# VectorE's work beside the expert loop in smaller pieces: norm in 14 slots instead of 7, routing in 30 instead of 20

## The chip, the cores and the metric

One core of one Trainium2 chip runs the whole program in one launch. The metric is the device time of one execution in microseconds (us); given are the median and the extremes of several runs. The engines are PE (TensorE, matmuls), DVE (VectorE), ACT (ScalarE), POOL (GpSimd) and SP (SyncE, which only issues transfers). Each works through its own list of instructions in order; semaphores alone tie the lists together.

## The reference

The input is x of 2 x 1024 tokens of 128 features. Four layers follow one another, and each adds to x:

```
x += attention_a(layernorm(x))   # full, 16 heads of 8, 1024 keys
x += experts(layernorm(x))
x += attention_b(layernorm(x))   # banded, 32 keys back
x += experts(layernorm(x))       # same weights

experts(x): shared = silu(x sg^T) * (x su^T) sd^T
  scores  = sigmoid(x gate^T) + gate_bias            # 64 experts, 8 groups of 8
  mask    = the 4 groups with the largest maximum
  comb    = the 6 largest masked scores, divided by their sum, 0 elsewhere
  routed  = sum over experts e of comb[e] * (silu(x eg[e]^T) * (x eu[e]^T)) ed[e]
```

Every token goes through every expert; `comb` is the weight, mostly zero. So what is called routing here is the making of the weights `comb` for 1024 tokens: norm, logits, two rounds of "keep the largest k, ties by position", and a normalisation.

## The kernel before, in words

The tokens are two batches of 1024 (8 tiles of 128 tokens, `TB = 8`). The 64 experts and 2 shared ones stand in 33 pairs (`PAIRS`). `experts` runs once per expert layer (names M1ex and M2ex) and is one loop over 132 steps q: step q works on pair q // 2 and on half a batch (512 tokens, c = q % 2); the first 66 steps (`HB`) are batch 0, the rest batch 1. In one step

- PE does `gate_up(q)`, 6 matmuls of 512 columns into two banks of a ring of three, and `down(q - 3)`, 3 more. `gate_up(q)` waits for `hid_ready` of step q - 2, since it writes the bank that DVE then has read;
- ACT does `silu(q)` and a cast to 16 bits (`high_part(q - 1)`);
- DVE does `times_up(q)` and `times_weight(q)` (the rows `ring` and `hid`), the second one with the weights of the pair (`cb`), which SP fetches per pair from the DRAM array `comb`;
- POOL makes the low half, `low`, from `hid` and `high`.

Beside the first 66 steps the same engines prepare batch 1: the attention's output projection, norm and routing. This work is written as generators, and each engine's loop calls `next(beside)` once per step, on DVE behind `times_weight(q)`. What a generator does between two `yield`s is called a **slot** or a **piece** here. The slots tie the engines together only by count: 13 slots for the projection (steps 0 to 12), then `NORM_SLOTS` and `ROUTE_SLOTS`. PE's transposes of the normed tiles are in the last two slots of the norm, POOL's reciprocal root in the slot in which DVE asks for it, PE's transposes of `comb` in the last two slots of the routing, DVE's last routing piece one slot ahead of them. In M1ex a second norm, of batch 0 for the next attention, is called from step 74 on (`AFTER`). Batch 1's weights are written to DRAM by `store_weights` on SP, inside SP's loop over pairs p, and pair 33 is the first that reads them. The same generators run without a loop, one piece straight after another, at the end of the first attention (on DVE) and in `first_batch` of the second expert layer.

Of the kernel before, what the change touches and what calls it, by code (L numbers as in the profile page):

```python
# [83 lines left out]
def attend_full(nc, env, tag):  # L84
# [10 lines left out]
    with ExitStack() as ctx:  # L95
# [566 lines left out]
def start(nc, env, d):  # L662
# [4 lines left out]
    with ExitStack() as ctx:  # L667
# [78 lines left out]
        def _(dve):  # L746
# [9 lines left out]
            for _ in range(3):  # L756
                next(norm)
# [312 lines left out]
def norm_of_batch_vector(dve, env, n, b, bank=None):  # L1070

    x = lambda t: env.x[:, TB * b + t, :]
    for t in range(TB):
        dve.bn_stats(n.stats[:, t, :], x(t)).then_inc(n.step, 1)
        if t == TB // 2 - 1:
            yield
    yield
# [4 lines left out]
    dve.tensor_scalar(n.ve[:, :], n.mv[:, :, 1], EPS, None, ALU.add).then_inc(n.var_ready, 1)
    yield
# [20 lines left out]
def norm_of_batch_gpsimd(pool, env, n):  # L1104


    for _ in range(3):
        yield
# [3 lines left out]
    for _ in range(4):  # L1112
# [101 lines left out]
def route_gpsimd(pool, env, n, q, b):  # L1214
# [18 lines left out]
def route_vector(dve, env, q):  # L1233
# [637 lines left out]
```

## Time and profile before

| | |
|---|---|
| median of 3 runs | 1254.93 us (1249.84 to 1260.67) |
| profiled execution, its own time | 1258.97 us |
| its span, first to last instruction | 1257.1 us |
| busy: PE, DVE, ACT, POOL | 1082.9, 960.0, 686.8, 423.0 us |
| mean granted clock of PE | 0.897 of full speed |
| M1ex loop | 453 to 752 us |
| M2ex loop | 966 to 1254 us |
| transfer of one pair's weights, issue to landing (median) | 4.0 us |

The profile lists what each engine did and when; a "granted clock" of 1.00 is 2.4 GHz, 0.50 is 1.2 GHz. Busy time is an average over stages with different limits: what the change is worth must be read inside the two expert loops. In a timeline row a bracket such as [0.36 <-ACT M1ex_sil L1648] says how long the engine had been idle before the instruction, and which instruction it had waited for.

### The profile page before, as it was taken

To read this page: it belongs to the slowest core of one execution; us is meant where nothing else is said; L and a number is where in the kernel's file an instruction comes from. 1 tells how busy PE (TensorE), PEld (TensorE's weight loads), DVE (VectorE), ACT (ScalarE), POOL (GpSimd) and SP (SyncE) were. 2 spreads that over 40 slices of the span, in tenths; PEclk is the share of its full clock that TensorE was granted. 3 is DMA by queue.
4 is the path that set the end of the run, shared out by engine and by line. 5 is a ranking of instruction groups with operands and counts; after the bars stand their busy time and mean duration, and the time that the engine had idled before them with its cause. 6 is when DMAs were issued, how large, how long until landed. Compare 5 with 4: busy or idle time off the path is not lost. (4 is left out here: it accounts for less than half of the span.)

```text
span 1257.1 us, 18664 instructions
## 1 busy us (share of the span) xinstructions
PE 1082.9 (86%) x6278; PEld 435.3 (35%) x6278; DVE 960.0 (76%) x2188; ACT 686.8 (55%) x1047; POOL 423.0 (34%) x352
## 2 busy tenths in 40 slices
PE   6586999999999988989989993688854988999998
PEld 4111222222222334434444441233342543444443
DVE  8599999999998567787767765777335768777775
ACT  2103787778777854656655651345512555666665
POOL 3004055322000124555545550000001555555654
PEclk8555999999999989999999996689755999999999
DMA  8220022202200144557747833121012646667662
GB/s 316 53 50 26 20 53 73 73 21 52 50 1 7 34 124 130 156 144 193 184 116 200 210 78 100 47 59 54 3 38 65 166 120 157 186 189 197 187 188 64
DMA packets 72903, 131.62 MB, mean 105 GB/s; under 512 B 13400, under 2 KB 48344, under 8 KB 72808
## 3 DMA queue, kind: packets, MB, share of 16 engines
q1 hardware_dynamic: 70320, 122.50, 36.6%
q10 hardware_dynamic: 2488, 7.93, 1.8%
q8 instruction: 50, 0.82, 0.3%
q14 instruction: 45, 0.37, 0.1%
HBM read 115.08 MB, written 14.91 MB: 103 GB/s over the span
## 5 line engine op out<-in xcount | busy, mean ns | idle before, releaser
L374 DVE TENSOR_REDUCE Aatt_mx<-Aatt_sc 128x1 f32<-128x512 f32 x512 | 317.7, 684 | 25.7 <-PE Aatt_sc L222 25.2
L325 ACT ACTIVATE Aatt_prob<-Aatt_st 128x1024 f32<-128x1024 f32 x256 | 247.7, 1022 | 77.4 <-PE Aatt_st L231 76.7
L222 PE MATMUL Aatt_sc<-ks,qs 48*128 48x512 bf16 x512 | 171.8, 430 | 42.8 <-DVE Aatt_mx L374 20.5
L1755 POOL TENSOR_TENSOR M1ex_low<-M1ex_hid,M1ex_high 128x512 f16<-128x512 f32 x132 | 153.6, 1164 | 149.8 <-ACT M1ex_high L1654 72.3
L1755 POOL TENSOR_TENSOR M2ex_low<-M2ex_hid,M2ex_high 128x512 f16<-128x512 f32 x132 | 153.6, 1164 | 136.5 <-PE M2ex_acc L1610 81.9
L1648 ACT ACTIVATE M2ex_sil<-M2ex_ring,unscale 128x512 f32<-128x512 f32 x132 | 90.7, 687 | 96.9 <-PE M2ex_ring L1593 96.8
L1648 ACT ACTIVATE M1ex_sil<-M1ex_ring,unscale 128x512 f32<-128x512 f32 x132 | 90.7, 687 | 95.7 <-PE M1ex_ring L1593 95.4
L242 PE MATMUL Aatt_pv<-Aatt_prob,vg 128*32 128x512 f32 x1024 | 141.0, 623 | 0.6 <-ACT Aatt_prob L325 0.6
L1692 DVE SCALAR_TENSOR_TENSOR M2ex_ring<-M2ex_ring,unscale,M2ex_sil 128x512 f32<-128x512 f32 x132 | 100.1, 758 | 48.8 <-ACT M2ex_sil L1648 44.6
L1692 DVE SCALAR_TENSOR_TENSOR M1ex_ring<-M1ex_ring,unscale,M1ex_sil 128x512 f32<-128x512 f32 x132 | 100.0, 757 | 48.5 <-ACT M1ex_sil L1648 44.0
L222 PEld LDWEIGHTS Aatt_sc<-ks,qs 48*128 48x128 bf16 x512 | 37.4, 95 | 240.0 <-DVE Aatt_mx L374 217.7
L231 PE MATMUL Aatt_st<-qs,ks 51*128 51x512 bf16 x512 | 106.7, 393 | 3.6 <-ACT Aatt_prob L325 2.6
L1702 DVE TENSOR_TENSOR M2ex_hid<-M2ex_ring,M2ex_cb 128x512 f32<-128x512 f32 x132 | 91.3, 692 | 15.5
L1702 DVE TENSOR_TENSOR M1ex_hid<-M1ex_ring,M1ex_cb 128x512 f32<-128x512 f32 x132 | 91.3, 692 | 15.5
L625 DVE CUSTOM_DVE_ANT_0 Batt_sc<-Batt_sc,mask 128x160 f32<-128x160 f32 (+1 forms) x256 | 74.3, 353 | 36.7 <-PE Batt_sc L515 36.7
L1654 ACT CAST M1ex_high<-M1ex_hid 128x512 f16<-128x512 f32 x132 | 80.5, 610 | 25.3 <-DVE M1ex_hid L1702 23.2
L1654 ACT CAST M2ex_high<-M2ex_hid 128x512 f16<-128x512 f32 x132 | 80.4, 609 | 18.4 <-DVE M2ex_hid L1702 17.0
L602 ACT ACTIVATE Batt_prob<-Batt_st 128x320 f32<-128x320 f32 x128 | 49.0, 435 | 55.9 <-PE Batt_st L566 55.9
L190 POOL COPY vg<-vn 128x256 f32<-128x256 f32 x8 | 3.2, 398 | 186.5 <-PE Aatt_pv L242 181.3
L1591 PE MATMUL M1ex_ring<-M_xh,M_wt 128*128 128x512 f16 x132 | 51.1, 387 | 10.5 <-DVE M1ex_hid L1702 5.5
L1591 PE MATMUL M2ex_ring<-M_xh,M_wt 128*128 128x512 f16 x132 | 50.7, 384 | 8.5 <-DVE M2ex_hid L1702 5.0
L515 PE MATMUL Batt_sc<-ks,qs 48*128 48x160 bf16 (+1 forms) x256 | 34.3, 267 | 22.7 <-DVE Batt_m L625 14.7
(423 smaller groups left out, 1863.4 us busy)
## 6 DMA issues: line engine op xcount, KB each, us to landing
M1ex_cb<-comb SPq DMA_DIRECT2D x130, 256.0 KB, 4.0
M2ex_cb<-comb SPq DMA_DIRECT2D x130, 256.0 KB, 3.9
M_wt<-wsplit SPq DMA_DIRECT2D x132, 192.0 KB, 3.9
wsplit<-split_cut SPq DMA_DIRECT2D x9, 704.0 KB, 4.5
qs<-stack SPq DMA_DIRECT2D x32, 96.0 KB
ks<-stack SPq DMA_DIRECT2D x30, 96.0 KB
split_raw<-in_wg_dram ACTq DMA_DIRECT2D x3, 704.0 KB, 7.0
split_raw<-in_wu_dram ACTq DMA_DIRECT2D x3, 704.0 KB, 13.3
```

The costliest lines, as they stand in the source:

```text
L222: pe.matmul(sc_bank(k, i)[:, :], qs[k][rows, jp, qt * P:(qt + 1) * P], ks[k][rows, jp, h * CH:(h + 1) * CH], start=True, stop=True).then_i ...
L231: mm = pe.matmul(st[jp][:, half, :], ks[k][rows, jp, kc * P:(kc + 1) * P], qs[k][rows, jp, qh * CH:(qh + 1) * CH], start=True, stop=True)
L242: mm = pe.matmul(pv[32 * j:32 * j + 32, :], vg[k][:, kc, j, :], prob[(2 * s + j % PAIR) % 4][:, j // PAIR, :], start=kc == 0, stop=kc == T ...
L325: act.activation(prob[e % 4][:, :, :].rearrange("p a c -> p (a c)"), st[pr][:, :, :].rearrange("p a c -> p (a c)"), ACT.Exp, scale=SCALE). ...
L374: dve.tensor_reduce(mx[k][:, m, part // 2:part // 2 + 1], sc_bank(k, i)[:, :], AX.X, ALU.max).then_inc(red_done, 1)
L625: ins = dve.tensor_tensor_reduce(scores, scores, mask_q[:, first:BAND], -1.0, -BARRED, ALU.add, ALU.min, accum_out=m1[k][:, j, qt:qt + 1])
L1591: pe.matmul(gate(q)[:, :], wt[k][:, 0, :], env.xh[:, cs], start=True, stop=False)
L1648: act.activation(sil[q % 2][:, :], gate(q)[:, :], ACT.Silu, scale=env.unscale[:, 0:1]).then_inc(sil_ready, 1)
L1654: act.copy(high[q % 3][:, :], hid[q % 3][:, :]).then_inc(high_ready, 1)
L1692: dve.scalar_tensor_tensor(up(q)[:, :], up(q)[:, :], env.unscale[:, 1:2], sil[q % 2][:, :], ALU.mult, ALU.mult).then_inc(up_ready, 1)
L1702: dve.tensor_tensor(hid[q % 3][:, :], up(q)[:, :], cb[k][:, c * CH:(c + 1) * CH], ALU.mult).then_inc(hid_ready, 1)
L1755: pool.tensor_tensor(low[q % 3][:, :], hid[q % 3][:, :], high[q % 3][:, :], ALU.subtract).then_inc(low_ready, 1)
```

## The change

DVE's pieces of norm and routing are cut smaller and stand in more slots; PE, ACT and POOL count to the new slots. POOL's root stays in slot 7, and DVE now takes it up one slot later, not in the same one. PE's transposes now stand two slots behind what they need, not one. The comparisons "greater", "equal" and the scan over experts are each split in two halves of 4 tiles. The end of the first attention keeps the old counts (7 and 20) on PE and ACT. On SP the store of batch 1's weights moves from pair 29 to just ahead of the fetch for pair 33. Core of the diff (calls that only pass the counts on are left out):

```diff
+OUT_SLOTS, NORM_SLOTS, ROUTE_SLOTS = 3 * ROUNDS_OUT + 1, 14, 30
+SHORT_NORM, SHORT_ROUTE = 7, 20
-OUT_SLOTS, NORM_SLOTS, ROUTE_SLOTS = 3 * ROUNDS_OUT + 1, 7, 20
@@ norm_of_batch_vector
         dve.bn_stats(n.stats[:, t, :], x(t)).then_inc(n.step, 1)
-        if t == TB // 2 - 1:
+        if t % 2:
             yield
-    yield
     dve.wait_ge(n.step, TB)
     for t in range(TB):
         dve.bn_aggr(n.mv[:, t, :], n.stats[:, t, :]).then_inc(n.step, 1)
+        if t == TB // 2 - 1:
+            yield
     dve.wait_ge(n.step, 2 * TB)
     dve.tensor_scalar(n.ve[:, :], n.mv[:, :, 1], EPS, None, ALU.add).then_inc(n.var_ready, 1)
     yield
+    yield
     dve.wait_ge(n.root_ready, 1)
...
     dve.wait_ge(n.step, 2 * TB + 3)
+    yield
     for t in range(TB):
...
-        if t in (1, 4):
+        if t % 2:
             yield
@@ norm_of_batch_gpsimd
-    for _ in range(3):
+    for _ in range(6):
         yield
     pool.wait_ge(n.var_ready, 1)
@@ route_gpsimd
-    for _ in range(ROUTE_SLOTS - 9):
+    for _ in range(16):
         yield
     pool.wait_ge(q.inv_ready, 1)
@@ route_vector: best() yields after 4 of its 8 dve.max; pick():
-        goes_on(dve.tensor_tensor(k.gt[:, :, :], values[:, :, :], wide(kth, n), ALU.is_gt))
-        yield
-        done(dve.tensor_tensor(k.eq[:, :, :], values[:, :, :], wide(kth, n), ALU.is_equal))
-        goes_on(dve.tensor_reduce(k.quota[:, :], k.above[:, :, 0:top], AX.X, ALU.add))
-        yield
-        done(dve.tensor_tensor_scan(flat(k.rank), flat(fresh), flat(k.eq), 0.0, ALU.mult, ALU.add))
+        for h in parts:
+            goes_on(dve.tensor_tensor(k.gt[:, h, :], values[:, h, :], wide(kth[:, h], n), ALU.is_gt))
+            yield
+        for h in parts:
+            goes_on(dve.tensor_tensor(k.eq[:, h, :], values[:, h, :], wide(kth[:, h], n), ALU.is_equal))
+            yield
+        dve.wait_ge(q.step, count[0])
+        done(dve.tensor_reduce(k.quota[:, :], k.above[:, :, 0:top], AX.X, ALU.add))
+        for h in parts:
+            goes_on(dve.tensor_tensor_scan(flat(k.rank[:, h, :]), flat(fresh[:, h, :]), flat(k.eq[:, h, :]), 0.0,
+                                           ALU.mult, ALU.add))
+            yield
         done(dve.tensor_scalar(k.quota[:, :], k.quota[:, :], -1.0, float(top), ALU.mult, ALU.add))
-        yield
         done(dve.tensor_tensor(k.keep[:, :, :], k.rank[:, :, :], wide(k.quota[:, :], n), ALU.is_le))
+        yield
         done(dve.tensor_tensor(k.keep[:, :, :], k.keep[:, :, :], k.eq[:, :, :], ALU.mult))
@@ experts, sync
                 sp.wait_ge(hid_ready, 2 * (p - CB_RING) + 2)
+                if p == PAIRS:
+                    store_weights(sp, env, q1, 1)
                 weights(p)
...
-                if p == PAIRS - 4:
-                    store_weights(sp, env, q1, 1)
```

DVE's list in M1ex, from the second group of `bn_stats` of the norm to the first normed tiles (`ring` and `hid` are the loop's own two operations, `r1`, `rstd` the steps behind POOL's root `r0`), before:

```order
L1074 BN_STATS M1exln_stats<-x_res 128x6 x4
L1692 SCALAR_TENSOR_TENSOR M1ex_ring1<-M1ex_ring1,unscale,M1ex_sil1 128x512
L1702 TENSOR_TENSOR M1ex_hid0<-M1ex_ring1,M1ex_cb2 128x512
L1080 BN_AGGR M1exln_mv<-M1exln_stats 128x2 x8
L1082 TENSOR_SCALAR M1exln_ve<-M1exln_mv 128x8
L1692 SCALAR_TENSOR_TENSOR M1ex_ring0<-M1ex_ring0,unscale,M1ex_sil0 128x512
L1702 TENSOR_TENSOR M1ex_hid1<-M1ex_ring0,M1ex_cb3 128x512
L1085 TENSOR_TENSOR M1exln_r1<-M1exln_r0 128x8
L1087 SCALAR_TENSOR_TENSOR M1exln_r1<-M1exln_r1,M1exln_ve 128x8
L1089 SCALAR_TENSOR_TENSOR M1exln_rstd<-M1exln_r1,M1exln_r0 128x8
L1092 TENSOR_SCALAR M1exln_xn<-x_res,M1exln_mv,M1exln_rstd 128x128 x2
```

and now, from the second half of the aggregation on:

```order
L1081 BN_AGGR M1exln_mv<-M1exln_stats 128x2 x4
L1085 TENSOR_SCALAR M1exln_ve<-M1exln_mv 128x8
L1703 SCALAR_TENSOR_TENSOR M1ex_ring0<-M1ex_ring0,unscale,M1ex_sil1 128x512
L1713 TENSOR_TENSOR M1ex_hid1<-M1ex_ring0,M1ex_cb4 128x512
L1703 SCALAR_TENSOR_TENSOR M1ex_ring2<-M1ex_ring2,unscale,M1ex_sil0 128x512
L1713 TENSOR_TENSOR M1ex_hid2<-M1ex_ring2,M1ex_cb0 128x512
L1089 TENSOR_TENSOR M1exln_r1<-M1exln_r0 128x8
L1091 SCALAR_TENSOR_TENSOR M1exln_r1<-M1exln_r1,M1exln_ve 128x8
L1093 SCALAR_TENSOR_TENSOR M1exln_rstd<-M1exln_r1,M1exln_r0 128x8
L1703 SCALAR_TENSOR_TENSOR M1ex_ring1<-M1ex_ring1,unscale,M1ex_sil1 128x512
L1713 TENSOR_TENSOR M1ex_hid0<-M1ex_ring1,M1ex_cb0 128x512
L1097 TENSOR_SCALAR M1exln_xn<-x_res,M1exln_mv,M1exln_rstd 128x128 x2
```

The root is asked for behind `ve`, and a whole step now stands between `ve` and `r1`; the normed tiles come in twos, a step later still.

DVE's list in M1ex round the scan (`rank`) over the experts, before:

```order
L1262 TENSOR_TENSOR M1exrt_experts_eq<-M1exrt_masked,M1exrt_experts_top8 128x512
L1263 TENSOR_REDUCE M1exrt_experts_quota<-M1exrt_experts_above 128x8
L1692 SCALAR_TENSOR_TENSOR M1ex_ring0<-M1ex_ring0,unscale,M1ex_sil0 128x512
L1702 TENSOR_TENSOR M1ex_hid1<-M1ex_ring0,M1ex_cb2 128x512
L1265 SCALAR_TENSOR_TENSOR M1exrt_experts_rank<-fresh,M1exrt_experts_eq 128x512
L1266 TENSOR_SCALAR M1exrt_experts_quota<-M1exrt_experts_quota 128x8
L1692 SCALAR_TENSOR_TENSOR M1ex_ring2<-M1ex_ring2,unscale,M1ex_sil1 128x512
L1702 TENSOR_TENSOR M1ex_hid2<-M1ex_ring2,M1ex_cb2 128x512
L1268 TENSOR_TENSOR M1exrt_experts_keep<-M1exrt_experts_rank,M1exrt_experts_quota 128x512
L1269 TENSOR_TENSOR M1exrt_experts_keep<-M1exrt_experts_keep,M1exrt_experts_eq 128x512
```

and now, from the first half of `eq` on:

```order
L1271 TENSOR_TENSOR M1exrt_experts_eq<-M1exrt_masked,M1exrt_experts_top8 128x256
L1703 SCALAR_TENSOR_TENSOR M1ex_ring2<-M1ex_ring2,unscale,M1ex_sil1 128x512
L1713 TENSOR_TENSOR M1ex_hid2<-M1ex_ring2,M1ex_cb3 128x512
L1271 TENSOR_TENSOR M1exrt_experts_eq<-M1exrt_masked,M1exrt_experts_top8 128x256
L1703 SCALAR_TENSOR_TENSOR M1ex_ring1<-M1ex_ring1,unscale,M1ex_sil0 128x512
L1713 TENSOR_TENSOR M1ex_hid0<-M1ex_ring1,M1ex_cb4 128x512
L1274 TENSOR_REDUCE M1exrt_experts_quota<-M1exrt_experts_above 128x8
L1276 SCALAR_TENSOR_TENSOR M1exrt_experts_rank<-fresh,M1exrt_experts_eq 128x256
L1703 SCALAR_TENSOR_TENSOR M1ex_ring0<-M1ex_ring0,unscale,M1ex_sil1 128x512
L1713 TENSOR_TENSOR M1ex_hid1<-M1ex_ring0,M1ex_cb4 128x512
L1276 SCALAR_TENSOR_TENSOR M1exrt_experts_rank<-fresh,M1exrt_experts_eq 128x256
L1703 SCALAR_TENSOR_TENSOR M1ex_ring2<-M1ex_ring2,unscale,M1ex_sil0 128x512
```

No piece now holds a whole scan, and `quota` (the small subtraction ahead of `keep`) has moved from the scan's piece to that of `keep`.

SP's list in M1ex round the store of batch 1's weights, before:

```order
L1548 DMA M1ex_cb<-comb 64x1024 [waits split_stored2]
L1548 DMA M1ex_cb<-comb 64x1024
L1426 DMA M_wt<-wsplit 128x768 [waits split_step]
L1210 DMA comb<-M1exrt_combT 66x512 [waits startqkv_v_done] x2
L1548 DMA M1ex_cb<-comb 64x1024 [waits split_stored2]
L1548 DMA M1ex_cb<-comb 64x1024
L1426 DMA M_wt<-wsplit 128x768 [waits split_step]
```

and now:

```order
L1559 DMA M1ex_cb<-comb 64x1024 [waits split_stored2]
L1559 DMA M1ex_cb<-comb 64x1024
L1437 DMA M_wt<-wsplit 128x768 [waits split_step]
L1212 DMA comb<-M1exrt_combT 66x512 [waits startqkv_v_done,split_stored2]
L1212 DMA comb<-M1exrt_combT 66x512 [waits startqkv_v_done]
L1559 DMA M1ex_cb<-comb 64x1024 [waits M1_comb_stored1]
L1559 DMA M1ex_cb<-comb 64x1024
L1437 DMA M_wt<-wsplit 128x768 [waits split_step]
L1559 DMA M1ex_cb<-comb 64x1024 [waits split_stored2]
```

The store stood several pairs ahead of the fetch that waits for it (`M1_comb_stored1`); now that fetch stands right behind it, with the weight matrices and all later pairs queued behind.

## Rows read from the trace of the kernel before

**Rows 1.** Busy time by stretch: us, PE, PEld, DVE, ACT, POOL, then clock, DMA.

```profile
487.07:557.51 70.44, 60.38 (x277) 27.21 (x276) 55.37 (x126) 38.09 (x62) 36.98 (x31) 0.95 0.51 140
502.20:505.90 3.70, 3.70 (x11) 1.43 (x11) 2.31 (x6) 1.35 (x4) 1.16 (x1) 0.50 0.67 194
582.77:606.08 23.31, 23.31 (x110) 10.55 (x109) 17.41 (x25) 14.31 (x25) 13.88 (x12) 1.00 0.73 187
624.43:645.75 21.32, 16.83 (x72) 7.55 (x71) 14.60 (x43) 9.88 (x17) 9.69 (x8) 0.92 0.49 131
999.51:1069.71 70.20, 60.02 (x277) 27.02 (x276) 55.34 (x126) 38.20 (x62) 36.97 (x31) 0.98 0.53 138
```

**Rows 2.** Timeline, DVE, undisturbed steps: start us, us, engine, line, operation.

```profile
581.72 0.69 DVE L1702 TENSOR_TENSOR M1ex_hid<-M1ex_ring,M1ex_cb 128x512 f32<-128x512 f32 x1
582.77 0.76 DVE L1692 SCALAR_TENSOR_TENSOR M1ex_ring<-M1ex_ring,unscale,M1ex_sil 128x512 f32<-128x512 f32 x1 [0.36 <-ACT M1ex_sil L1648]
```

**Rows 3.** Timeline, PE and POOL in the same step.

```profile
583.14 0.38 PE L1591 MATMUL M1ex_ring<-M_xh,M_wt 128*128 128x512 f16 x1
...
583.32 1.16 POOL L1755 TENSOR_TENSOR M1ex_low<-M1ex_hid,M1ex_high 128x512 f16<-128x512 f32 x1 [0.79 <-PE M1ex_acc L1610]
```

**Rows 4.** Chain of waits, second expert stage: start us, us, what.

```profile
1018.51 0.44 PE M2ex_side L1133 x4
...
1022.84 0.84 PE M2ex_side L1173 x8
```

**Rows 5.** Timeline, DVE, the norm of the first expert stage.

```profile
488.55 0.86 DVE L1074 BATCH_NORM_STATS2 M1exln_stats<-x_res 128x6 f32<-128x128 f32 x4
489.32 0.74 DVE L1692 SCALAR_TENSOR_TENSOR M1ex_ring<-M1ex_ring,unscale,M1ex_sil 128x512 f32<-128x512 f32 x1
...
498.94 0.17 DVE L1085 TENSOR_TENSOR M1exln_r<-M1exln_r 128x8 f32<-128x8 f32 x1 [3.57 <-POOL M1exln_r L1110]
...
499.55 0.60 DVE L1092 TENSOR_SCALAR M1exln_xn<-x_res,M1exln_mv,M1exln_rstd 128x128 f32<-128x128 f32 x2
```

**Rows 6.** Timeline, POOL and PE, in the same norm.

```profile
497.27 1.64 POOL L1110 TENSOR_TENSOR M1exln_r<-M1exln_ve,minus_half 128x8 f32<-128x8 f32 x1
...
499.95 0.73 PE L1133 MATMUL M1ex_side<-ident,M1exln_xn 128*128 128x128 f32 x2 [2.97 <-DVE M1exln_xn L1092]
```

**Rows 7.** Timeline, DVE and POOL round the experts' scan, first expert stage.

```profile
542.43 1.04 POOL L1225 TENSOR_TENSOR M1exrt_weighted<-M1exrt_masked,M1exrt_inv 128x512 f32<-128x512 f32 x1
...
542.78 1.78 DVE L1265 TENSOR_TENSOR_SCAN M1exrt_experts_rank<-fresh,M1exrt_experts_eq 128x512 bf16<-128x512 bf16 x1
...
543.70 1.80 POOL L1755 TENSOR_TENSOR M1ex_low<-M1ex_hid,M1ex_high 128x512 f16<-128x512 f32 x1 [0.22 <-POOL M1exrt_weighted L1225]
...
544.59 0.94 DVE L1266 TENSOR_SCALAR M1exrt_experts_quota<-M1exrt_experts_quota 128x8 f32<-128x8 f32 x1
```

**Rows 8.** By line, DVE: duration ns min/median/max, first and last start, shape.

```profile
L1265 DVE TENSOR_TENSOR_SCAN Aattrt_groups_rank<-fresh_g,Aattrt_groups_eq x1: 280/280/280, 436.7 to 436.7; 128x64 bf16<-128x64 bf16 x1
...
L1265 DVE TENSOR_TENSOR_SCAN Aattrt_experts_rank<-fresh,Aattrt_experts_eq x1: 1216/1216/1216, 443.3 to 443.3; 128x512 bf16<-128x512 bf16 x1
...
L1260 DVE TENSOR_TENSOR M1exrt_groups_gt<-M1exrt_gs,M1exrt_groups_top x1: 220/220/220, 523.1 to 523.1; 128x64 bf16<-128x64 f32 x1
...
L1260 DVE TENSOR_TENSOR M1exrt_experts_gt<-M1exrt_masked,M1exrt_experts_top x1: 685/685/685, 538.4 to 538.4; 128x512 bf16<-128x512 f32 x1
```

**Rows 9.** Timeline, DVE and PE, further pieces of the routing.

```profile
517.76 0.84 DVE L1278 SCALAR_TENSOR_TENSOR M1exrt_sc<-M1exrt_sc,gate_b 128x512 f32<-128x512 f32 x1
...
552.45 0.63 PE L1180 MATMUL M1ex_side<-ident,M1exrt_comb 128*66 128x128 f32 x4 [1.05 <-DVE M1exrt_comb L1303]
```

**Rows 10.** Timeline, SP: the weights' store and their reads.

```profile
448.78 0.90 SPq L1210 DMA_DIRECT2D comb<-split_raw  x2
...
453.08 1.15 SPq L1548 DMA_DIRECT2D M1ex_cb<-comb  x2
...
592.12 1.08 SPq L1548 DMA_DIRECT2D M1ex_cb<-comb  x2
```

More of the change, by code:

```diff
@@ L255, in first_batch @@
                 yield from out_tensor(pe, env, o, bank, 0)
-                yield from norm_of_batch_tensor(pe, env, n1, bank)
-                yield from route_tensor(pe, env, n1, q1, bank)
+                yield from norm_of_batch_tensor(pe, env, n1, bank, SHORT_NORM)
+                yield from route_tensor(pe, env, n1, q1, bank, SHORT_ROUTE)
             def second_batch():
@@ L334, in first_batch @@
             def first_batch():
-                for _ in range(OUT_SLOTS + NORM_SLOTS):
+                for _ in range(OUT_SLOTS + SHORT_NORM):
                     yield
-                yield from route_scalar(act, env, n1, q1, bank, 0, copies=False)
+                yield from route_scalar(act, env, n1, q1, bank, 0, copies=False, slots=SHORT_ROUTE)
             beside = first_batch()
@@ L1104, in norm_of_batch_gpsimd @@
 def norm_of_batch_gpsimd(pool, env, n):
-    for _ in range(3):
+    for _ in range(6):
         yield
@@ L1111, in norm_of_batch_gpsimd, with norm_of_batch_scalar @@
     pool.wait_ge(n.root_ready, 1)
-    for _ in range(4):
+    for _ in range(NORM_SLOTS - 6):
         yield
-def norm_of_batch_scalar(act, env, n, bank):
-    for _ in range(5):
+def norm_of_batch_scalar(act, env, n, bank, slots=NORM_SLOTS):
+    for _ in range(slots - 2):
         yield
@@ L1123, in norm_of_batch_scalar, with norm_of_batch_tensor @@
         yield
-def norm_of_batch_tensor(pe, env, n, bank):
-    for _ in range(5):
+def norm_of_batch_tensor(pe, env, n, bank, slots=NORM_SLOTS):
+    for _ in range(slots - 2):
         yield
@@ L1161, in route_buffers, with route_tensor @@
     return q
-OUT_SLOTS, NORM_SLOTS, ROUTE_SLOTS = 3 * ROUNDS_OUT + 1, 7, 20
-def route_tensor(pe, env, n, q, bank):
+def route_tensor(pe, env, n, q, bank, slots=ROUTE_SLOTS):
     for c in range(2):
@@ L1174, in route_tensor @@
         mm.then_inc(q.lg_done, 1)
-    for _ in range(ROUTE_SLOTS - 4):
+    for _ in range(slots - 4):
         yield
@@ L1182, in route_tensor, with route_scalar @@
         yield
-def route_scalar(act, env, n, q, bank, b, copies=True):
+def route_scalar(act, env, n, q, bank, b, copies=True, slots=ROUTE_SLOTS):
     for c in range(2):
@@ L1196, in route_scalar @@
                    scale=0.5).then_inc(q.sig_ready, 1)
-    for _ in range(ROUTE_SLOTS - 4):
+    for _ in range(slots - 4):
         yield
@@ L1228, in route_gpsimd @@
     pool.wait_ge(q.weighted_ready, 1)
-    for _ in range(7):
+    for _ in range(ROUTE_SLOTS - 18):
         yield
@@ L1290, in route_vector @@
     yield
-    best(of_experts, q.masked)
-    yield
+    yield from best(of_experts, q.masked)
     done(dve.tensor_reduce(q.total[:, :], of_experts.top8[:, :, 0:TOPK], AX.X, ALU.add))
@@ L1297, in route_vector @@
     yield
-    yield from pick(of_experts, q.masked, E, TOPK, env.fresh)
+    yield from pick(of_experts, q.masked, E, TOPK, env.fresh, HALVES)
     yield
@@ L1304, in route_vector @@
                       ALU.mult).then_inc(q.comb_ready, 1)
-    yield
-    yield
     yield
```

20 lines of the change are left out of this document (13 added, 7 removed).

## The prediction

> **What bounds the kernel now.** I read the busy times by stretch first. In an undisturbed part of an expert loop, 582.77 to 606.08 us, PE is busy for all 23.31 us at clock 1.00; these are 12 steps, so a step takes 1.94 us and PE sets it [rows 1]. Then the stretches that this change touches. Steps 13 to 39 of M1ex, norm and routing of batch 1, take 70.44 us, in M2ex 70.20 us; 27 steps at 1.94 are 52.4. PE has work of its own there that stays: two lots of four transposes of normed tiles at 0.44, two lots of logits at 0.84 [rows 4], and two lots of transposes of the weights, which I take at 0.44 too: 3.4 us. So **14.6 us in M1ex and 14.3 in M2ex are stalls**. Steps 74 to 80 of M1ex, the second norm, take 21.32 us [rows 1]; less 7 steps (13.6) and 0.9 for transposes, 6.8 are stalls. Together 35.7 us can be won, no more.
>
> Next, DVE's timeline, for what makes them. The step with four bn_stats (0.86) goes from 487.07 to 489.32, 2.25 us, and DVE doesn't idle behind it [rows 1, 5]. So DVE's own two operations with their gaps take 1.40, and **a piece of up to 0.54 us is free**; a longer one puts DVE behind by the rest. There is a reserve as well: hid ends at 582.41 (581.72 + 0.69), and PE, which waits for it, starts the bank's matmuls at 583.14 [rows 2, 3]. Allowing 0.05 for the semaphore, DVE may lag **0.68 us** before PE stands still, and it catches up 0.54 in each empty slot.
>
> The large stalls of before are then plain. In the norm DVE idles 3.57 us for POOL's root [rows 5]; PE stands 2.97 us before its transposes, behind the same root [rows 6], and is at clock 0.50 from 502.20 to 505.90, 3.70 us [rows 1]. In the routing the piece with the scan takes 1.78 + 0.94 [rows 7], and PE waits another 1.05 for the last piece [rows 9].
>
> **The change, norm.** Pairs of bn_stats (half of 0.86) and halves of the aggregation are under 0.54: free. The root: POOL starts it behind its low part of the same step. In an undisturbed step low ends at 583.32 + 1.16 = 584.48 [rows 3], 2.07 us behind the end of hid; the root takes 1.64 [rows 6], so it is there 3.71 behind that hid. Before, DVE came for it in the same step; now it comes a step, 1.94, later, and still idles 1.8. From r1 to the first normed tile it needs 0.61 (498.94 to 499.55 [rows 5]): a piece of 2.4, a lag of 1.87, a stall of 1.19 with the reserve gone. Four pieces of two normed tiles at 0.60 [rows 5] lag 0.06 each; the tail of POOL's low, 0.13 into each, may add as much, so 0.4. PE's transposes stand two slots behind their tiles: no wait there, and with PE idle for 1.2 instead of 3 us I expect no fall of the clock. Norm: **1.6 us left** of its stalls, three times.
>
> **The change, routing.** Half a comparison is estimated between 0.220 us at 64 elements and 0.685 at 512 [rows 8]: 0.42 at 256. Half a scan, between 0.280 and 1.216 [rows 8]: 0.68. Longest slots, as lag over 0.54 with 0.05 for a wait inside: the scores (0.84 [rows 9]) 0.36, group maxima 0.15 and masking 0.2 (as wide as the full comparison, 0.69), the four steps to the inverse 0.3, then free slots up to there and back to a lag of some 0.55. Now POOL forms the weighted scores, 1.04 us [rows 7], two steps behind the inverse, beside the first half of "equal". What that does rows 7 tell: weighted ends at 543.47, and the scan, started at 542.78, takes 1.78 instead of the 1.216 that it takes alone [rows 8], which is 0.56 more, as if it began at 543.34; POOL's low then takes 1.80 instead of 1.16; and quota, 0.94 for 8 elements, ends at 545.53, when low ends (545.50). They take turns, whole instructions at a time. So this slot is 1.0 longer than its 0.54: stall 0.9. The Trainium skill says the same in "SBUF — State Buffer", section "Who interferes with whom": VectorE and GpSimd share one pair of ports, and whoever issues first keeps it for the whole instruction. By that rule the sum holds as it stands; if they shared the bandwidth instead, that slot would cost about 0.1, and the result would be 1.6 us lower. Then, at full lag: maxima of the quota with half a scan (0.20 + 0.68) 0.35, second half 0.15, quota with keep (0.17 + 0.69) 0.45, the last piece 0.1. Routing: **1.9 left**, twice. The transposes of the weights, two slots behind, wait for nothing.
>
> **Sum.** First loop 14.6 − 1.6 − 1.9 = 11.1; second loop 14.3 − 3.5 = 10.8; second norm 6.8 − 1.6 = 5.2: 27.1 us. Against it: where DVE runs these steps alone, twice (end of the first attention, first_batch), three operations are now two each. Two halves of a comparison are 0.84 in duration against 0.685, of scans 1.36 against 1.216; most of the surplus overlaps, I take 0.3 us a pass, all on the path. The Trainium skill, "VectorE: DVE Perf Modes", section "The TRN2 errata", speaks against this change: each instruction pays a fixed latency, so tiles should be kept to 512 elements or more; with its formula, (N + 151) / 0.96 ns, an estimate for a half is 0.424 us. With that the three split pairs cost 0.47 a pass, and the result would be 0.3 us higher. At the start of the program DVE's order stays as it was. Net **−26.5 us**.
>
> The store on SP costs nothing in my sum. Its cover: the fetch for pair 33 is issued at 592.12 and its weights are used in step 66, 16.8 us later, of which the transfer takes 4.0. From store to the first read behind it took 4.3 us (448.78 to 453.08) [rows 10], so 8.5 are left, and the queue behind it (a matrix, then pair 34) is 5 pairs ahead.
>
> Against the profiled execution's own 1258.97 us the sum gives 1232.5. That execution is 4.0 above the median of the runs shown, 1254.93; so I forecast **1228.4 us**.
>
> **Rivals.**
> - *A (0.68), the forecast.* Own range 1223 to 1234, from what the residues could be: 7.0 of the 8.6 us left rest on the lag sums, and the three runs spread by 5 either way.
> - *B (0.12), the root stays dear.* If DVE lags when it asks, POOL lags with it, and the wait keeps more than 1.8 of its 3.57. For: POOL does low first, whatever the slot. Against: six pieces ahead of it are free. Price: up to 1.8 for each of three norms, 5.3, and if PE's stall then again lowers the clock, 1.85 each (3.70 us at half speed [rows 1]): 1234 to 1239.
> - *C (0.08), turns at the port everywhere.* DVE has some 14 pieces with two inputs per routing. If each met a POOL instruction as the scan did (0.6 to 0.8), 10 us per loop return: 1248. Against: in an undisturbed step low covers 583.32 to 584.48, and pieces stand mostly outside it. Meeting half of them gives 1238.
> - *D (0.08), nothing is left.* Pieces hide wholly, the root included: all 35.7 less 0.6: 1219.8. Against: the root's wait can't be shorter than low and root together.
> - *E (0.02), slower than before: the late store.* All of SP's list stands behind it. It decides from 12.8 us between store and first read; to return all 26.5 us it needs 13.3 more per loop, 26.1. At 30 it gives 1228.4 + 2 × 17.2 = 1262.8. Seen: 4.3.
> - *F (0.02), no effect.* If the slots of PE waited where DVE waits no more, 1250 to 1255. The list of DVE does change as the diff says, so this asks for a cause I don't see.
>
> **Numbers.** Less than 1% (12.5 us) can't be told from no change. Faster by more: A, B, D and over half of C, 0.93; within 1%: the rest of C, and F, 0.05; slower 0.02. The range for 8 in 10 takes A with its spread, B's lower half and D's edge: 1221 to 1238.
>
> **What would show it.** Right: steps 13 to 69 of each loop at 1.94 but for PE's own work; DVE's wait for the root at 1.8; clock 1.00 in the norm; no idle of PE before transposes of tiles or weights; the scan's halves near 0.68 and "quota" at 0.17; "equal", first half, near 1.4 for its turn behind weighted; cb of pair 33 landed before step 66. Wrong: a root wait near 3.5, a clock of 0.5 behind it, pieces lengthened beside low, or DVE idle for cb at step 66.

## The result, and the profile after

The changed kernel takes **1239.34 us** (median of 4 runs, 1234.83 to 1241.40) where the kernel before, run beside it, takes 1257.8: a ratio of 0.985, 95% interval 0.981 to 0.989. It is faster, as forecast, but by 18.5 us and not by 26.5, and the time lies 1.3 us above the range. The profiled execution took 1239.16 us with a span of 1237.3, 19.8 less than before.

First the stretches, by the windows view (columns as in [rows 1]). I cut each kernel at the first and the last of the 132 `ring` operations of an expert loop, since these are the loop's own clock. The kernel before, first loop, the stretch between the loops, second loop:

```profile
456.15:748.92 292.77, 277.35 (x1300) 130.61 (x1299) 223.40 (x396) 170.70 (x285) 157.74 (x135) 0.98 0.61 162
748.92:968.70 219.78, 143.94 (x1372) 67.71 (x1371) 122.35 (x680) 76.24 (x180) 12.55 (x15) 0.72 0.16 47
968.70:1247.35 278.65, 268.10 (x1268) 125.73 (x1267) 212.65 (x357) 164.15 (x275) 156.11 (x134) 0.99 0.63 167
```

and the changed kernel: the same three, then steps 13 to 26 (norm) and 27 to 56 (logits and routing) of M1ex, steps 74 to 87 (second norm), and the norm and the routing in M2ex:

```profile
455.68:734.96 279.28, 272.78 (x1300) 129.59 (x1299) 223.52 (x399) 170.74 (x285) 157.02 (x135) 0.99 0.67 170
734.96:957.83 222.87, 145.12 (x1373) 68.65 (x1372) 122.60 (x684) 76.22 (x180) 12.29 (x15) 0.71 0.16 46
957.83:1227.57 269.74, 266.19 (x1268) 125.23 (x1267) 212.26 (x361) 163.97 (x275) 155.45 (x134) 0.99 0.67 172
486.49:518.41 31.92, 29.93 (x136) 13.63 (x135) 25.59 (x56) 17.90 (x31) 17.78 (x15) 0.95 0.67 163
518.41:581.17 62.76, 61.87 (x296) 28.60 (x295) 53.90 (x107) 40.41 (x66) 38.16 (x33) 1.00 0.66 172
615.07:645.50 30.43, 28.32 (x135) 13.21 (x134) 25.49 (x57) 18.23 (x31) 17.80 (x15) 1.00 0.65 167
988.64:1020.55 31.91, 29.93 (x136) 13.62 (x135) 25.72 (x57) 17.90 (x31) 17.76 (x15) 0.95 0.61 161
1020.55:1082.95 62.40, 61.78 (x296) 28.61 (x295) 53.89 (x107) 40.39 (x66) 38.18 (x33) 1.00 0.67 173
```

The loops lost 13.5 and 8.9 us, **22.4 together, where 27.1 were forecast**; the stretch between them, where only the 0.3 us of one serial pass was charged, took 3.1 more. Inside the loops a step at PE's pace is 1.9425 us (23.31 us for 12 steps in [rows 1]). A norm has 14 steps and 0.88 us of PE's own work (its transposes), a routing 30 steps and 2.56 us (logits and transposes). With these taken off, the stalls that remain are: norms 31.92 − 27.2 − 0.88 = 3.84 in M1ex, 3.83 in M2ex, second norm 2.36; routing 62.76 − 58.3 − 2.56 = 1.9 and 1.6. So the routing is as forecast (3.5 for 3.8). **The norms keep 10.0 where 4.8 were forecast.**

Why, the timelines show. Changed kernel, DVE, the norm of M1ex at the root (answers to [rows 5]):

```profile
503.42 0.17 DVE L1089 TENSOR_TENSOR M1exln_r<-M1exln_r 128x8 f32<-128x8 f32 x1 [1.75 <-POOL M1exln_r L1115]
503.62 1.02 DVE L1091 SCALAR_TENSOR_TENSOR M1exln_r<-M1exln_r,M1exln_ve 128x8 f32<-128x8 f32 x1
504.68 0.17 DVE L1093 SCALAR_TENSOR_TENSOR M1exln_rstd<-M1exln_r 128x8 f32<-128x8 f32 x1
```

POOL, the same place (answers to [rows 6]):

```profile
501.75 1.64 POOL L1115 TENSOR_TENSOR M1exln_r<-M1exln_ve,minus_half 128x8 f32<-128x8 f32 x1
503.47 1.16 POOL L1766 TENSOR_TENSOR M1ex_low<-M1ex_hid,M1ex_high 128x512 f16<-128x512 f32 x1
```

The wait for the root is 1.75, as forecast (1.8; before 3.57). But the second small step behind it takes 1.02 us for 8 elements. In the same trace it takes 0.17 in the five norms outside the expert loops, where POOL has no `low` to start, and 1.02 in all three inside. It starts 0.15 behind POOL's `low` and ends (504.64) when `low` ends (504.63): POOL, freed of the root at the same moment as DVE, starts its late `low` at once, and the step waits for it to end. What PE makes of it:

```profile
504.13 0.38 PE L1621 MATMUL M1ex_acc<-M1ex_low,M_wt 128*128 128x512 f16 x1
506.50 0.39 PE L1602 MATMUL M1ex_ring<-M_xh,M_wt 128*128 128x512 f16 x1 [1.99 <-DVE M1ex_hid L1713]
...
507.19 0.63 PE L1607 MATMUL M1ex_ring<-M_xh,M_wt 128*128 128x512 f16 x1
...
509.75 0.63 PE L1602 MATMUL M1ex_ring<-M_xh,M_wt 128*128 128x512 f16 x1
...
510.57 0.38 PE L1604 MATMUL M1ex_ring<-M_xh,M_wt 128*128 128x512 f16 x1
```

PE stands 1.99 us, not 1.19, and then its matmuls take 0.63 instead of 0.38 from 507.19 to 510.17: the clock is at its lower level for some 3.4 us. In the second norm PE stood even longer, and the clock stayed at 1.00:

```profile
635.19 0.38 PE L1602 MATMUL M1ex_ring<-M_xh,M_wt 128*128 128x512 f16 x1 [2.10 <-DVE M1ex_hid L1713]
635.41 0.38 PE L1603 MATMUL M1ex_ring<-M_xl,M_wt 128*128 128x512 f16 x1
```

The routing, DVE at the experts' comparison and scan (answers to [rows 7, 8]):

```profile
559.30 0.48 DVE L1271 TENSOR_TENSOR M1exrt_experts_eq<-M1exrt_masked,M1exrt_experts_top 128x256 bf16<-128x256 f32 x1
...
561.17 1.04 DVE L1271 TENSOR_TENSOR M1exrt_experts_eq<-M1exrt_masked,M1exrt_experts_top 128x256 bf16<-128x256 f32 x1
...
563.85 0.69 DVE L1276 TENSOR_TENSOR_SCAN M1exrt_experts_rank<-fresh,M1exrt_experts_eq 128x256 bf16<-128x256 bf16 x1
...
567.98 0.16 DVE L1279 TENSOR_SCALAR M1exrt_experts_quota<-M1exrt_experts_quota 128x8 f32<-128x8 f32 x1
```

and POOL there:

```profile
559.46 1.23 POOL L1227 TENSOR_TENSOR M1exrt_weighted<-M1exrt_masked,M1exrt_inv 128x512 f32<-128x512 f32 x1
560.77 2.46 POOL L1766 TENSOR_TENSOR M1ex_low<-M1ex_hid,M1ex_high 128x512 f16<-128x512 f32 x2
```

The long turn came, but a step later than forecast and shorter: the first half of "equal" was already under way when `weighted` started, and it is the second half that waited, behind the `low` that `weighted` had delayed. That half takes 1.04, 0.5 over the free 0.54, where the prediction had near 1.4, 1.0 over it.

The store, SP's queue (answers to [rows 10]):

```profile
582.75 0.71 SPq L1212 DMA_DIRECT2D comb<-M1exrt_combT  x2
585.45 1.09 SPq L1559 DMA_DIRECT2D M1ex_cb<-comb  x2
...
587.21 1.08 SPq L1559 DMA_DIRECT2D M1ex_cb<-comb  x2
```

From the store to the first read behind it are 2.7 us; the fetch after it follows 1.76 us behind, so the queue catches up. DVE doesn't wait for the weights: its idle time before step 66 is 0.39 us, spent on ACT, and 0.36 to 0.39 before the steps beside it.

### The profile page after: what moved, and what is told of

The parts are those of the page before. It is cut to its first block and busy times, and to the rows that moved or that the text cites. A ratio compares the mean times of both kernels' runs of the same rounds, so it can differ in the third digit from the quotient of the medians.

```text
span 1237.3 us, 18676 instructions
## 1 busy us (share of the span) xinstructions
PE 1075.6 (87%) x6278; PEld 433.5 (35%) x6278; DVE 960.3 (78%) x2200; ACT 686.7 (56%) x1047; POOL 421.1 (34%) x352
## 5 line engine op out<-in xcount | busy, mean ns | idle before, releaser
L222 PE MATMUL Aatt_sc<-ks,qs 48*128 48x512 bf16 x512 | 171.4, 428 | 43.2 <-DVE Aatt_mx L374 19.8
L602 ACT ACTIVATE Batt_prob<-Batt_st 128x320 f32<-128x320 f32 x128 | 49.1, 436 | 57.8 <-PE Batt_st L566 57.8
L515 PE MATMUL Batt_sc<-ks,qs 48*128 48x160 bf16 (+1 forms) x256 | 34.5, 273 | 22.4 <-DVE Batt_m L625 14.1
```

The lines of the kernel that those rows point to most:

```text
L222: pe.matmul(sc_bank(k, i)[:, :], qs[k][rows, jp, qt * P:(qt + 1) * P], ks[k][rows, jp, h * CH:(h + 1) * CH], start=True, stop=True).then_i ...
```

## The experiments

Two theories of where the missing 5 us of the loops are. *R*: the price of the root is not only DVE's wait for it, but the turn that its followers lose to POOL's delayed `low`, and the fall of the clock that the longer stall brings at times; keep DVE away until root and `low` are through, and it is gone. *H*: the pieces themselves are too many or too long (halving, the collision in the routing). What a kernel's loops take is the sum of its two loop rows as above: before 571.4, changed 549.0.

**e1: the changed kernel again.**

> The changed kernel once more, on the same chip as the next three and in the same rounds. It separates what the change did inside the expert loops from what varies elsewhere: the stretch between the two expert loops (last ring row of M1ex to first ring row of M2ex), whose code the change hardly touches, was 219.8 us in the trace of before and 222.9 in the changed kernel's. If the 3.1 us are a variation of that stretch from execution to execution, its length differs again here and among the next three; if the change causes them (through the state in which the second attention starts), it stays near 222.9 here. The expert loops are expected within 0.5 us of the first trace (279.3 and 269.7 us from first to last ring row).

Measured: 1235.99 us, ratio 0.986 (0.982 to 0.990); loops 546.9. Norm of M1ex, and PE behind the same idle time:

```profile
494.02:524.39 30.37, 28.38 (x136) 13.04 (x135) 25.49 (x57) 18.25 (x31) 17.80 (x15) 1.00 0.63 166
```

```profile
514.03 0.39 PE L1602 MATMUL M1ex_ring<-M_xh,M_wt 128*128 128x512 f16 x1 [1.99 <-DVE M1ex_hid L1713]
...
514.90 0.38 PE L1608 MATMUL M1ex_ring<-M_xl,M_wt 128*128 128x512 f16 x1
```

The same kernel, the same 1.99 us of idle time, and no fall: 30.37 instead of 31.92. So **the fall costs 1.5 us a norm, and the same code sometimes has it and sometimes not**. The loops are 2.1 us shorter than in the first trace, outside the 0.5 expected: 3.1 less for the two falls, and 1.0 more because PE's clock was still at its lower level when the loops began (four matmuls at 0.63 us in step 0 of M2ex). The stretch between the loops took 219.63 us, not 222.87, so the 3.1 us by which it was longer in the first trace come and go in the same kernel. Without a fall a norm keeps 2.30, against 1.6 forecast; the 0.7 left over answers to the lost turn (1.02 − 0.17 = 0.85).

**e2: DVE comes for the root a step later still.**

```diff
     yield
     yield
+    yield
     dve.wait_ge(n.root_ready, 1)
-..., NORM_SLOTS, ... = ..., 14, ...
+..., NORM_SLOTS, ... = ..., 15, ...
```

> One more empty slot between var_ready and DVE's wait for POOL's root, 15 slots for the norm. Theory 1: the stalls left in the norms (3.8, 3.8 and 2.4 us) come from DVE arriving 1.75 us before the root, then having its second small step (1.02 instead of 0.17 us) held by POOL's low, and in two norms PE's clock at 0.5 behind the 2 us in which it stood. Then with one more slot the idle of 1.75 and the 1.02 are gone, PE doesn't stand, the clock stays at 1.00, and each norm keeps 0.5 or less: 8.5 us faster than the changed kernel, ratio to the kernel before about 0.978. Rival: DVE's lag, not its early arrival, sets the wait (POOL's root comes later too when the slots move); then the idle stays near 1.75 and the time that of the changed kernel.

Measured: 1229.31 us, ratio 0.979 (0.976 to 0.982); loops 543.6. Of DVE and POOL at the root:

```profile
510.66 0.69 DVE L1714 TENSOR_TENSOR M1ex_hid<-M1ex_ring,M1ex_cb 128x512 f32<-128x512 f32 x1
511.26 1.15 DVE L1090 TENSOR_TENSOR M1exln_r<-M1exln_r 128x8 f32<-128x8 f32 x1
512.45 1.08 DVE L1092 SCALAR_TENSOR_TENSOR M1exln_r<-M1exln_r,M1exln_ve 128x8 f32<-128x8 f32 x1
513.56 0.17 DVE L1094 SCALAR_TENSOR_TENSOR M1exln_rstd<-M1exln_r 128x8 f32<-128x8 f32 x1
```

```profile
509.51 1.64 POOL L1116 TENSOR_TENSOR M1exln_r<-M1exln_ve,minus_half 128x8 f32<-128x8 f32 x1
511.23 2.27 POOL L1767 TENSOR_TENSOR M1ex_low<-M1ex_hid,M1ex_high 128x512 f16<-128x512 f32 x2
```

DVE's idle time is gone, and the kernel is 6.7 us faster than e1 beside it, where 8.5 were expected. My expectation of at most 0.5 us left per norm is missed: by the 15 steps of each norm it is 1.5 (31.55, 31.61 and 31.48 us, less 29.14 and 0.88). POOL now owes two `low`s, and two small steps wait for one each, ending at 512.41 and 513.53 where the `low`s end at about 512.4 and 513.5. The turn, not the wait for the root alone, is the price.

**e3 and e4: the norm's part alone, the routing's part alone** (e3: the norm of after, with routing and store of before; e4: the routing of after, with norm and store of before).

> The norm as in the changed kernel (14 slots), the routing and the weights' store as before (20 slots). Theory 1: the parts add up, the norm took its stalls from 7.3, 7.0 and 6.8 to 3.8, 3.8 and 2.4 us: 11.1 us faster than before (0.991). Rival: the routing takes over DVE's lag from the norm, so that the norm alone gives less (under 8 us) and its routing stretch is longer than the 48.7 us that it took before.

> The routing as in the changed kernel (30 slots, halves), the norm as before (7 slots), the weights' store at its place of before, which is just late enough. Theory 1: the routing stalls go from 7.3 us in each loop to 1.9 and 1.6, and its two passes outside the loops get 0.2 us longer each: 10.7 us faster than before (0.9915). Rival: the turns at the port eat the gain, under 6 us.

Measured: e3 1242.99 us, 0.991 (0.988 to 0.994); e4 1246.94 us, 0.994 (0.991 to 0.996). Their two loops each, e3 and then e4:

```profile
454.83:738.25 283.42, 273.96 (x1300) 129.84 (x1299) 224.92 (x395) 170.90 (x285) 157.75 (x135) 0.99 0.65 168
...
956.48:1230.84 274.36, 267.50 (x1268) 125.77 (x1267) 213.58 (x357) 163.94 (x275) 156.12 (x134) 0.99 0.64 169
```

```profile
453.99:741.81 287.82, 276.48 (x1300) 130.63 (x1299) 221.75 (x398) 171.42 (x285) 157.01 (x135) 0.98 0.63 165
...
958.72:1233.18 274.46, 268.40 (x1268) 126.21 (x1267) 211.28 (x360) 164.56 (x275) 155.38 (x134) 0.99 0.65 169
```

13.6 and 9.1 us: together 22.7, the 22.4 of the whole change. Expected were 11.1 and 10.7 for the kernels' times; the ratios say 11.5 and 7.8. Neither part hides the other; but that the sum is met this closely is chance in part, since falls of PE's clock lie differently in each execution. e3 has none in its norms, but one in each routing, behind an idle time of 2.29 us (2.07 and no fall in the kernel before), so that its 20 routing steps take 48.8 and 49.1 us (48.7 before); e4's norms take 0.9 and 1.6 us longer than before's, with PE's mean clock in M2ex's at 0.85 and not 0.92.

**e5: two steps later.** As e2 with one more `yield`, and `NORM_SLOTS` 16.

> A second empty slot ahead of DVE's wait for the root, 16 slots for the norm. In the run with one such slot DVE no longer idled, but its first two small steps, each with two SBUF inputs, took 1.15 and 1.08 us where 0.17 is their own, while POOL, put back by its root, made two low parts in a row (2.27 us); 1.0 us of stall was left per norm. Theory 1: the two engines take turns at a port, so a slot later, with POOL's arrears gone, the two steps take at most 0.3 each, nothing is left of the stall, and the loops take 1.0 us less for each of the three norms, 3 in all (543.6 us for the two loops becomes 540.6). Rival: the small steps are slow because they follow the root closely or read what POOL wrote last; then they stay near 1.1 us each wherever they stand behind a low part.

Measured: **1224.83 us, ratio 0.974 (0.971 to 0.977)**; loops 538.7. DVE at the root, and the norms of M1ex (first, second) and M2ex:

```profile
506.53 0.29 DVE L1091 TENSOR_TENSOR M1exln_r<-M1exln_r 128x8 f32<-128x8 f32 x1
506.85 0.17 DVE L1093 SCALAR_TENSOR_TENSOR M1exln_r<-M1exln_r,M1exln_ve 128x8 f32<-128x8 f32 x1
507.05 0.17 DVE L1095 SCALAR_TENSOR_TENSOR M1exln_rstd<-M1exln_r 128x8 f32<-128x8 f32 x1
```

```profile
487.54:515.22 27.68, 27.68 (x132) 12.82 (x131) 24.68 (x56) 17.36 (x29) 17.75 (x15) 1.00 0.71 178
...
611.91:639.58 27.67, 27.67 (x132) 12.85 (x131) 24.70 (x57) 17.36 (x29) 17.74 (x15) 1.00 0.68 183
977.78:1005.52 27.74, 27.74 (x132) 12.81 (x131) 24.75 (x57) 17.47 (x29) 17.79 (x15) 1.00 0.67 180
```

PE is busy for all of 27.68 us. These rows hold 14 of the norm's 16 steps; all 16 take 31.96, 31.95 and 31.95 us, which is 16 × 1.9425 and the 0.88 of the transposes: no stall in any norm. This is R, shown: one waiting point moved, nothing shortened, and the loops give up 10.3 us more than in the changed kernel's own profile. 10.0 of these are the norms', 6.9 as stalls and 3.1 as falls of the clock. Against e1, which had no fall in its norms, the loops give up 8.2. The same pieces are there as before, so H has no share in the norms. The expectation had 540.6 for the loops, since it took 1.0 us a norm for what was left in e2; it was 1.5. The rival is out: the two small steps, which read the same root, take 0.29 (it ends with POOL's second `low`) and 0.17 here, and in the norms outside the loops they follow the root at once and take 0.17.

**e6: whole comparisons and scans, with an empty slot where the second half was.** For the 512-wide pick only:

```diff
-for h in parts: gt, eq, rank each on [:, h, :], then yield
+gt, eq, rank each whole, then yield, yield
```

> The changed kernel with greater, equal and the scan over experts in one piece each, in the slot of their first half, an empty slot in place of the second. It tells the halving from the spreading. Theory 1: only lag beyond the reserve costs; one scan of 1.2 us with the 0.2 of its neighbour is 0.9 over the free 0.54, two halves 0.5 together: each loop 0.5 to 1.0 us longer between steps 40 and 57 (1.8 us of stalls becomes 2.3 to 2.8), and the routing outside the loops 0.2 shorter, twice: total 1 us slower or no difference. Rival: the halves are what made the gain; then the scan's stall of before comes back, 2 us or more per loop.

Measured: 1230.05 us, ratio 0.978 (0.975 to 0.981); loops 546.4, like e1's 546.9. The scan whole in one piece took 1.39:

```profile
564.04 1.39 DVE L1280 TENSOR_TENSOR_SCAN M1exrt_experts_rank<-fresh,M1exrt_experts_eq 128x512 bf16<-128x512 bf16 x1
```

Over the 30 routing steps the two loops need 62.50 and 62.81 us, in e1 62.75 and 62.40. So in the wide comparisons and the scan the halves win nothing that an empty slot doesn't: it is the room that pays.

**e7: the kernel before, with the store moved as in the change.**

> The kernel before, with only the weights' store moved as in the change (from pair 29 to just ahead of the fetch for pair 33). My sum has it at nothing: store and wait 4.3 us, transfer 4.0 us, 16.8 us of room. Expected: ratio 1.000, no idle of DVE ahead of step 66, both loops within 0.3 us of 292.8 and 278.7. Rival (the late store): the queue behind it is late for steps 66 to 69, DVE idles there, 1 us or more per loop.

Measured: 1257.0 us, ratio 0.999 (0.996 to 1.002); loops 571.5. The store and its first read:

```profile
590.62 0.71 SPq L1210 DMA_DIRECT2D comb<-M1exrt_combT  x2
593.31 1.09 SPq L1548 DMA_DIRECT2D M1ex_cb<-comb  x2
```

The store is free. When it would not be (rival E's point) wasn't tried.

**e8: e5 and empty slots in the routing** behind the second half of "equal" and of the scan (32 routing slots).

> The kernel with the root's two extra slots, and besides two empty slots in the routing: behind the second half of equal (which POOL's turn makes 1.0 us) and behind the second half of the scan; 16 and 32 slots. Theory 1: each empty slot lets DVE catch up 0.54 us, so 1.1 of the 1.8 us of stalls of each loop's routing goes: 2 us for both loops less than the run before with 16 and 30 slots; the copies of the weights stand in steps 59 and 60, the first fetch of batch 1 comes 8.3 us behind them, which is still ahead of step 66. Against the kernel before: ratio 0.973 to 0.977. Rival: the later store now makes DVE wait at step 66; then the ratio is that of 16 and 30 slots or above it, and an idle time stands ahead of step 66.

Measured: **1221.14 us, ratio 0.971 (0.967 to 0.974)**, the lowest median; but loops 538.6, as e5's 538.7, where 2 us less were expected. The routings did get shorter, from 1.6 us of stalls in e5 to 1.2, in each loop; 0.6 of that was lost again at the start of the M2ex loop, where four matmuls of step 0 ran at the lower clock, as in e1. Why the routings gained 0.3 each and not 1.1, DVE shows:

```profile
565.32 0.89 DVE L1280 TENSOR_TENSOR_SCAN M1exrt_experts_rank<-fresh,M1exrt_experts_eq 128x256 bf16<-128x256 bf16 x1
...
571.13 0.56 DVE L1285 TENSOR_SCALAR M1exrt_experts_quota<-M1exrt_experts_quota 128x8 f32<-128x8 f32 x1
```

The scan's half and `quota`, 0.69 and 0.16 in the changed kernel, now start while `low` runs: the empty slots shifted the pieces into it. DVE doesn't idle for weights at step 66, so the rival is out. The 3.7 us between the medians of e5 and e8 aren't in the loops, and their ranges overlap (1221.5 to 1230.3, 1216.9 to 1228.6).

**e9, e10: the changed kernel and e6 again, on one chip.** The medians of the changed kernel had gained less than its loops.

> The changed kernel a third time, since its median so far gained less than its loops: two profiled executions show both expert loops together 22.4 and 24.5 us shorter than before, but the medians say 17.6 to 18.9 us (0.985 and 0.986). Theory 1 (chance in the stretches that the change doesn't touch, which took 213 to 223 us between the loops over nine profiled executions): loops again at 547 to 549 us together, and the ratio now nearer to the loops' gain, 0.980 to 0.983. Theory 2 (something in most executions of this kernel that the two profiles caught only in part, such as the fall of PE's clock behind the root, 1.5 us each): ratio again 0.985 to 0.986, and 5 us slower than the kernel with whole operations run beside it.

> The kernel with whole comparisons and scans and an empty slot behind each, again, on the same chip as the changed kernel. Its loops took 546.4 us, those of the changed kernel 546.9 and 549.0, while their medians stood at 0.9777 and 0.986 against the kernel before. Theory 1 (chance): both ratios come within 0.003 of each other. Theory 2 (halves cost something outside the loops' profiled executions): 0.005 or more between them again.

Measured: e9 1235.58 us, 0.983 (0.979 to 0.987), loops 549.0; e10 1231.63 us, 0.980 (0.977 to 0.984), loops 547.9. The two ratios are 0.003 apart, where 0.008 had been; that favours chance, without settling it. The profile of e10 shows what the chance is made of. The stretch between the loops, and the second norm:

```profile
736.33:948.97 212.64, 136.23 (x1372) 63.96 (x1371) 122.23 (x681) 76.39 (x180) 12.55 (x15) 0.78 0.17 48
...
614.60:646.85 32.25, 29.91 (x135) 13.73 (x134) 25.58 (x56) 18.02 (x31) 17.78 (x15) 0.95 0.58 158
```

Between the loops, in code that takes no part in the change but for one serial pass, this execution needs 212.64 us at a mean clock of 0.78, the changed kernel's first profile 222.87 at 0.71, with 136.23 and 145.12 us of PE busy for 1372 and 1373 recorded matmuls. Over all twelve profiled executions that stretch runs from 212.6 to 222.9 us, and its length follows the clock: 0.71 to 0.73 in the four longest (219.6 to 222.9), 0.75 to 0.78 in the four shortest (212.6 to 214.6). The same code in that stretch has it too: 219.78 us in the kernel before and 213.37 in e7; 222.87, 219.63 and 218.55 in the changed kernel.

## Why the prediction was right, and where it failed

*What bounds, and what can be won.* Right. PE's pace in a step is unchanged, and e5, which has no stall in its norms, shows that the norms' share of the stalls counted from [rows 1] was all there to be won. Of the routings' share every run left some; e8 the least, 1.2 us a loop.

*The root's wait* (1.8 forecast): right, 1.75. With it "rival B", a wait near 3.5, is out; that the time came to lie at B's upper end is chance, though a stall that lowers the clock, as B has it, was part of it. (The section on the change says that the root "stays" in slot 7. It moved: in the kernel before POOL had 3 slots ahead of it and made it in slot 4, where DVE came for it; now POOL has 6 ahead and DVE comes in slot 8.)

***The norm, "1.6 us left": the step that failed.*** Measured 3.84, 3.83 and 2.36. Two terms were missing. First, 2.4 was taken for DVE's piece "from r1 to the first normed tile" with the small steps at 0.17 each. I had read from [rows 7] that DVE's instructions with two inputs and POOL's take turns, whole instructions at a time, and charged it to the routing, where wide operations meet; I did not ask it of three steps of 8 elements, which come at the one moment when POOL is certain to start a `low`. In the kernel before there was no such `low`: DVE waited in the same step, had given POOL nothing since, and its steps took 0.17 each, as this view of DVE and POOL shows:

```profile
499.14 0.17 DVE L1087 SCALAR_TENSOR_TENSOR M1exln_r<-M1exln_r,M1exln_ve 128x8 f32<-128x8 f32 x1
```

```profile
502.45 1.16 POOL L1755 TENSOR_TENSOR M1ex_low<-M1ex_hid,M1ex_high 128x512 f16<-128x512 f32 x1 [3.54 <-issue]
```

The very step that the change puts between `ve` and `r1` makes the `low` that then stands in the way. Price: 0.7 in each norm, 2.1 together (e1 without a fall: 2.30 each). The rule in the Trainium skill, "SBUF — State Buffer", section "Who interferes with whom", which the prediction used, names no least size for it; the 1.02 us of an 8-element step agrees. Second, "with PE idle for 1.2 instead of 3 us I expect no fall of the clock": PE idled 1.99 (0.85 of it from the step of 1.02), and the clock fell in two of three norms in the result's own profile, 1.5 us each, 3.1 together. 2.1 + 3.1 is the 5.2 that the norms' 10.0 exceeds 4.8 by.

*The routing, 1.9 left:* right in size, 1.9 and 1.6, but not in its parts, so that luck has a share. The turn behind `weighted` was to put its slot 1.0 over the free 0.54; it was 0.5 over, on the second half of "equal" (1.04) and not on the first (0.48). By PE's own steps it lost 0.4 us ahead of that turn, 0.3 to it, and 1.3 behind the pieces of scan, `keep` and `comb`. By shared bandwidth, the prediction's alternative, 0.1 would have been paid for the turn. The row shows a whole turn: the first of POOL's two `low`s ends at about 561.93 (560.77 and 1.16), the half of "equal" that began at 561.17 ends at 562.21. Scan halves 0.69 and 0.68, `quota` 0.16, and no wait of PE before its transposes: as forecast. "Rival C", turns everywhere, is out.

Rivals D, nothing left, and F, no effect, are out as well: 13.5 us of stalls were left, and the loops lost 22.4. But D was only two slots away for the norms: e5 hides the root and its steps wholly.

*The serial passes, +0.3 each:* the passage from `sc` to `comb` in the pass between the loops grew from 12.46 to 12.63 us, 0.2. Half comparisons measure 0.41 to 0.42 each there, but for the second half of "greater", which takes 1.26 beside POOL's `weighted` (before, the whole "equal" took 1.53 beside it). The Trainium skill, "VectorE: DVE Perf Modes", section "The TRN2 errata", gives 0.424 by its formula, and these rows agree; but the second half of "equal" begins 0.34 behind the first, which takes 0.41, so most of the surplus is hidden, and the 0.47 a pass worked out from that formula is the farther one.

*The store, 0:* right (e7, and no wait at step 66 in the result).

*From the sum to the time.* The loops were 4.7 us short of the forecast, and the profiled execution 6.7 (1239.16 for 1232.5): the other 2.0 are the 3.1 of the stretch between the loops, less the 0.6 that was charged for the serial passes, less 0.5 by which the first loop began sooner. The last 4 of the 10.9 us between 1228.4 and 1239.34 are the step from profile to median: the profile of before stood 4.0 above the median of its first three runs, but only 1.2 above the 1257.8 of the runs beside the result, and that of the changed kernel stood at its own median. The series of e1 and e9 gave 1236.0 and 1235.6. The range took a clock fall at the root only for the case of a dear root. That the forecast's own stall could bring one was left out, and with 3.1 us for that the range would have reached 1241.

*What stays open.* By the ratios the changed kernel gains 18 to 21 us, its loops 22.4 to 24.5; e5 and e2 gain by the ratios what their loops gain (32.9 and 32.7; 26.6 and 27.8). The intervals, 4 to 5 us to either side, cover it; its cause isn't shown.

## What to carry to other kernels

When a wait for another engine is made shorter, look at what that engine does the moment it is done, and whether your next instruction shares a port with it: the step behind the wait can cost as much as the wait. Coming two steps later (e5) cost nothing and took 8 to 10 us more out of the loops. And cut pieces to get room, not for the cutting: behind the wide comparisons and the scan an empty slot did the same as a halved operation, and every slot added shifts the pieces against the other engine's rhythm, so look at the shifted ones again.

## What the runs showed of the hardware

- A DVE instruction on 128x8 with two inputs waits for POOL's 1.16 us instruction to end like a wide one: 1.02, 1.08 and 1.15 us instead of 0.17 (result, e2). `quota`, a small step with one input, was held too: 0.94 in [rows 7], 0.56 in e8, 0.16 alone. The loop's own `ring` and `hid`, which read `ring` and so have an input in PSUM, were never held: the longest of 264 each took 0.76 and 0.69 us, in the changed kernel as in e8.
- PE's clock went down to its lower level behind idle time of 1.99 us in M1ex in the changed kernel and in e9, and not behind the same 1.99 us in e1; behind 2.10 us it stayed up in all of these, and behind 2.34 us in the second norm it fell in e10 but not in e3 and e6. In the routing it stayed up behind 2.07 us (before, e7) and fell in both loops of e3 behind 2.29. Over the six profiled executions with this form of the norm it fell in 5 of 18 norms, for 1.5 to 1.6 us each time. The Trainium skill, "TensorE: Matmul & The Clock Gate", section "What's actually happening", calls the ramp, the slow matmuls before the clock has risen, variable from run to run for the same kernel. The starts of the loops agree: in step 0 of M2ex four matmuls took 0.63 us in e1 and none in e9, which is the same kernel.
- In stages where PE is busy for only two thirds of the time, as between the loops, the clock is worth up to 10 us from execution to execution (212.6 to 222.9 over all kernels, 213.4 to 219.8 over two executions of the same code there), more than most single steps of a change like this one.
